# Split 16-bit operands for half of the weighing units, one key distance for every tile, and x1 traffic issued by ScalarE

## The reference, cut to what matters

```python
x = x + attention(ln_channels(x))       # x is (8, 128, 56, 56): 7x7 neighbourhood attention, 16 heads of 8
t = to_tokens(x)
t = t + moe(ln_tokens(t))               # 8 experts, the best 2 by a softmax router, 128 -> 512 -> 128, relu
x = from_tokens(t, x)

# attention, for each pixel and head, over the 49 keys of its clamped 7x7 window:
logits = q . k + rpb[relative row, relative column]
out    = sum(softmax(logits) * v)
y      = out @ proj_w.T + proj_b
```

## Time and profile before

| | us |
|---|---|
| median of 3 runs (3019.34 to 3025.69) | 3022.98 |
| the profiled execution | 3022.68 |
| its span, first to last instruction | 3020.9 |
| busy in the span: PE, PEld | 2688.8, 2395.9 |
| busy in the span: DVE, ACT, POOL | 2269.4, 2114.3, 1583.9 |
| attention | from about 100 to 2250 |
| experts, then combine | from 2250 to 2890, and to the end |

### The profile page before, as it was taken

One profiled execution on the slowest core, in us unless ns is written; L12 is line 12 of the kernel. 1 busy time (PEld: TensorE's weight loads), 2 busy tenths in 40 slices (PEclk: granted clock), 3 DMA queues, 4 the chain that ended last, 5 costly groups with the idle time before them and its releaser, 6 DMA issues. The chain is left out here.

```text
span 3020.9 us, 112796 instructions
## 1 busy us (share of the span) xinstructions
PE 2688.8 (89%) x31346; PEld 2395.9 (79%) x31451; DVE 2269.4 (75%) x12559; ACT 2114.3 (70%) x5724; POOL 1583.9 (52%) x2025
## 2 busy tenths in 40 slices
PE   4789999999999999999999999999939999999733
PEld 2789999899989998999899989999936766776522
DVE  2668888788878887888788868888857888888655
ACT  1567878787878886887787868888847777777500
POOL 2135555455545554555455545555565777777600
PEclk9999999999999999999999999999969999999855
DMA  2665666555546664656566645566645444444399
GB/s 48 153 122 124 129 124 123 112 122 127 126 102 130 124 124 102 130 128 124 101 127 128 129 99 124 125 125 129 132 91 105 97 94 97 97 94 97 101 323 322
DMA packets 714047, 378.50 MB, mean 125 GB/s; under 512 B 422528, under 2 KB 669984, under 8 KB 713504
## 3 DMA queue, kind: packets, MB, share of 16 engines
q1 hardware_dynamic: 660704, 235.97, 40.3%
q10 hardware_dynamic: 24192, 81.67, 9.5%
q0 software_dynamic: 28608, 54.48, 6.1%
HBM read 233.43 MB, written 98.11 MB: 110 GB/s over the span
## 5 line engine op out<-in xcount | busy, mean ns | idle before, releaser
L1061 ACT ACTIVATE pr<-sc,nmx 128x100 f32<-128x100 f32 x3136 | 923.9, 369 | 61.9 <-DVE nmx L678 60.9
L962 POOL TENSOR_TENSOR oml<-om 128x256 f16<-128x256 f32 x784 | 479.6, 612 | 907.3 <-DVE om L708 890.4
L533 PE MATMUL bank<-vwin,pt 100*128 100x65 f32 x6272 | 806.2, 272 | 36.3 <-DVE om L708 28.1
L678 DVE CUSTOM_DVE_ANT_0 sc<-bank,near 128x100 f32<-128x100 f32 x3136 | 633.5, 257 | 253.7 <-PE bank L511 207.8
L533 PEld LDWEIGHTS bank<-vwin,pt 100*128 100x128 f32 x6272 | 773.4, 194 | 54.3 <-ACT pt L1069 39.5
L511 PE MATMUL bank<-kimg,held 128*128 (+2 forms) x9408 | 628.2, 216 | 40.9 <-issue 22.9
L511 PEld LDWEIGHTS bank<-kimg,held 128*128 128x128 bf16 (+1 forms) x9408 | 561.3, 100 | 88.3 <-issue 56.7
L1069 ACT ACTIVATE pt<-bank 100x512 f32<-100x512 f32 x784 | 460.6, 587 | 223.5 <-PE bank L520 208.8
L1367 POOL DMA_INDIRECT yrows<-ye,meta x420 | 449.2, 1070 | 154.6 <-issue 109.8
L930 POOL DMA_INDIRECT xrows<-rows,idx x448 | 433.9, 969 | 114.9 <-issue 75.5
L520 PE MATMUL bank<-cst_sb,pr 128*100 128x128 f32 x3136 | 477.1, 275 | 0.0
(11 more groups left out here) (133 smaller groups left out, 3366.8 us busy)
## 6 DMA issues: line engine op xcount, KB each, us to landing
vwin<-v_pix SPq DMA_DIRECT2D x1120, 60.5 KB
near<-bias_rows ACTq DMA_DIRECT2D x112, 600.0 KB, 4.7
y<-yrows SPq DMA_DIRECT2D x112, 224.0 KB, 4.3
held<-qring SPq DMA_DIRECT2D x896, 14.0 KB
v_pix<-vrow SPq DMA_DIRECT2D x56, 225.8 KB
xin<-in_x SPq DMA_DIRECT2D x56, 224.0 KB
xres<-in_x SPq DMA_DIRECT2D x112, 112.0 KB
x<-xres SPq DMA_DIRECT2D x112, 112.0 KB
```

The costliest lines, as they stand in the source:

```text
L533: mm = pe.matmul(ps_av[m % 2][:, 2 * t + blk, :], pt[:, m % 2, 2 * t + blk, :], vwin[:, st, 2 * u + t, 64 * blk:64 * blk + 65], start=True ...
L678: i = v.tensor_tensor_reduce(out=sc[:, ring(m, par), k, :], in0=ps_s[m % 2][:, k, :], in1=near[:, st, ct, k, :], scale=-1.0, scalar=-MASKE ...
L962: g.tensor_tensor(oml[:, st, u], om[:, st, u], om_h[:, st, u], ALU.subtract).then_inc(s["oml_done"], 1)
L1061: i = a.activation(pr[:, r, k, :], sc[:, r, k, :], ACT.Exp, bias=nmx[:, r, k:k + 1], scale=-1.0)
```

## The change

- `SPLIT` = (0, 3, 4, 5, 7, 10, 12): for these 7 of 14 units `weigh` does 12 matmuls with 16-bit operands instead of 4 in fp32: high x high, high x low, low x high. The high part of `pt` is read in place (every second 16-bit word). The low part `pl` is a subtraction on POOL, `split_t`, after `t_evict`.
- The low part of v is made on DVE by the new `a_v_l` at m = 12, after ACT's eviction of the rows, and stored beside the fp32 row: a pixel has 194 words (VP) instead of 129 (VW) in `v_pix` and `vwin`. `v_out`, for which `store_v` and the next `a_mean` wait, now comes from DVE.
- L_V, L_P, L_H and L_F are one unit later (5, 6, 7, 8), so the folds are at m = 0 and 7 and the projections at m = 2 and 9.
- All tiles take their keys from column 4 t - 3; what lies outside the image is masked, and `kimg` and `v_pix` have 4 zero pixels at either end. A strip's `windows` is ten DMAs of 14 tiles.
- exp is written in place in `sc`; `pr` is gone, and `add_bias` waits for the transposes of four units before.
- `store_x1`, `load_res` and `load_tokens` move from SP's queue to ACT's, at m = 4, 7, 11 and 13. SP's `spread_q` comes ahead of `load_x` and `windows(J, 1)`.
- The router's `gapr` moves from DVE to POOL, and four of the indirect DMAs move by one m.

The diff, cut to its core:

```diff
-L_T, L_V, L_P, L_H, L_F = 3, 4, 5, 6, 7
+L_T, L_V, L_P, L_H, L_F = 3, 5, 6, 7, 8
+SPLIT = (0, 3, 4, 5, 7, 10, 12)
+VP = VW + VW // 2 + 1
-WIN_DMAS = 16 * (KW + 2)
+WIN_DMAS = 16 * KW
...
                     for kr in range(KW):
-                        src = bass.AP(v_pix.tensor, at + (kr * W + 1) * VW, [[VW, KW], [TS * VW, NTILE - 2], [1, VW]])
-                        sp.dma_start(vwin[kr * KW:(kr + 1) * KW, st, 1:NTILE - 1], src).then_inc(s[f"v_in{st}"], 16)
-                    for t, c0 in ((0, 0), (NTILE - 1, W - KW)):
-                        src = bass.AP(v_pix.tensor, at + c0 * VW, [[W * VW, KW], [VW, KW], [1, VW]])
-                        sp.dma_start(vwin[:, st, t], src).then_inc(s[f"v_in{st}"], 16)
+                        src = bass.AP(v_pix.tensor, at + kr * W * VP, [[VP, KW], [TS * VP, NTILE], [1, VP]])
+                        sp.dma_start(vwin[kr * KW:(kr + 1) * KW, st], src).then_inc(s[f"v_in{st}"], 16)
...
 def weigh(J, m, par):
+                    if m in SPLIT:
+                        pe.wait_ge(s["t_out"], len(SPLIT) * J + SPLIT.index(m) + 1)
+                    else:
+                        pe.wait_ge(s["th_done"], n + 1)
...
+                            if m in SPLIT:
+                                p_h, p_l = pt_h[:, m % 2, 2 * t + blk, :], pl[:, m % 2, 2 * t + blk, :]
+                                v_h, v_l = vwin_h[:, st, 2 * u + t, cols], vwin_l[:, st, 2 * u + t, cols]
+                                for k, (a_, b_) in enumerate(((p_h, v_h), (p_h, v_l), (p_l, v_h))):
+                                    mm = pe.matmul(at_, a_, b_, start=k == 0, stop=k == 2)
...
+                def a_v_l(I):
+                    v.wait_ge(s["v_h"], I + 1)
+                    for blk in range(2):
+                        cols = slice(65 * blk, 65 * blk + 64)
+                        i = v.tensor_tensor(vrow_l[:, :, cols],
+                                            ps_a[0:HALF, :].rearrange("p (n c) -> p n c", n=NROW)[:, :, 64 * blk:64 * blk + 64],
+                                            vrow_h[:, :, cols], ALU.subtract)
+                    i.then_inc(s["v_out"], 1)
...
-                LATE_STEPS = {9: a_q_l, 10: a_k_l}
+                LATE_STEPS = {9: a_q_l, 10: a_k_l, 12: a_v_l}
...
+                def split_t(J, m, par):
+                    n = UPP * J + m
+                    g.wait_ge(s["th_done"], n + 1)
+                    g.tensor_tensor(pl[:, m % 2], pt[:, m % 2], pt_h[:, m % 2], ALU.subtract).then_inc(s["t_out"], 1)
...
                             if reached(J, m, L_H):
                                 split_l(*back(J, m, par, L_H))
+                            if reached(J, m, L_T) and (m - L_T) % UPP in SPLIT:
+                                split_t(*back(J, m, par, L_T))
...
+                            elif m == 4:
+                                store_x1(J - 1, 0)
+                            elif m == 7:
+                                load_res(J, 0)
+                            elif m == 11:
+                                store_x1(J - 1, 1)
+                            elif m == 13:
+                                load_res(J, 1)
+                                load_tokens(J - 1, 1 - par)
```

More of the change, by code:

```diff
@@ L383, in body @@
                     more = not (isinstance(J, int) and J == PAIRS - 1)
-                    if not early(J, 1):
-                        store_x1(J - 1, 0)
+                    if more:
+                        spread_q(J + 1, 1 - par)
                     if fetch:
@@ L389, in body @@
                     if more:
[L390 to L394, removed]
                         windows(J + 1, 0, tail)
-                    load_res(J, 1)
-                    if not early(J, 1):
-                        load_tokens(J - 1, 1 - par)
                     if I is not None:
@@ L622, in _ @@
                 v.memset(qexp[:, 1].rearrange("p s t h q -> p (s t h q)"), 0.0).then_inc(s["zeroed"], 1)
+                v.memset(vrow_l[:, :, 64:65], 0.0)
+                v.memset(vrow_l[:, :, VW:VW + 1], 0.0)
                 v.memset(vrow[:, :, 64:65], 1.0).then_inc(s["pad_zero"], 1)
+                for part in range(2):
+                    for col in (0, EDGE + IMG):
+                        i = v.memset(kimg[:, part, col:col + EDGE], 0.0)
+                i.then_inc(s["k_edge"], 1)
                 v.memset(ones_b[:], 1.0)
@@ L743, in rank @@
                     i.then_inc(s["r_top"], 1)
+                    if not early(c, 1):
+                        v.wait_ge(s["r_gapr"], c)
                     v.tensor_tensor(gap[:], top[:, :, 1], top[:, :, 0], ALU.subtract).then_inc(s["r_gap"], 1)
@@ L918, in root @@
                     g.tensor_tensor(nmr[:, par], nm[:], rs[:, par], ALU.mult).then_inc(s["r_nmr"], 1)
+                    g.wait_ge(s["r_gap"], c + 1)
+                    if not early(c, 1):
+                        g.wait_ge(s["r_eg"], 2 * c)
+                    g.tensor_tensor(gapr[:], gap[:], rs[:, par], ALU.mult).then_inc(s["r_gapr"], 1)
                 def scatter(c, par, j, n):
@@ L982, in _ @@
                     split_l(*back(PAIRS, m, PAIRS % 2, L_H))
+                    if m < L_T and (m - L_T) % UPP in SPLIT:
+                        split_t(*back(PAIRS, m, PAIRS % 2, L_T))
                 places_ = sorted(SCATTERS)
@@ L1046, in near_bias, with load_res, store_x1, load_tokens @@
                     a.dma_start(near[:, st].rearrange("p c a k -> p (c a k)"), src).then_inc(s[f"near_in{st}"], 16)
+                def load_res(J, st):
+                    b = J // NPAIR
+                    if not (isinstance(J, int) and J == 0):
+                        a.wait_ge(s[f"x1_store{st}"], 16 * J)
+                    src = bass.AP(x.tensor, b * (C * IMG) + (J % NPAIR) * PAIR + st * STRIP, [[IMG, C], [1, STRIP]])
+                    a.dma_start(xres[:, st, :], src).then_inc(s[f"xres_in{st}"], 16)
+                def store_x1(J, st):
+                    a.wait_ge(s["proj_out"], 2 * J + st + 1)
+                    a.dma_start(x1[:, bass.ds(J * PAIR + st * STRIP, STRIP)], xres[:, st, :])\
+                        .then_inc(s[f"x1_store{st}"], 16)
+                def load_tokens(Q, par):
+                    if not early(Q, 2):
+                        a.wait_ge(s["r_logit"], Q - 1)
+                    a.dma_start(xt[:, par, :], x1[:, bass.ds(Q * PAIR, PAIR)]).then_inc(s[f"r_x{par}"], 16)
                 def exps(J, m, par):
```

75 lines of the change are left out of this document (41 added, 34 removed).

## The result

The changed kernel takes 3196.7 us, the median of 4 runs (3174.72 to 3211.15). The kernel before, on the same chip, takes 3024.34 (3019.34 to 3038.62). The ratio is 1.054 [1.049, 1.059] (these two medians alone give 1.057): 5% slower, where 2906 was forecast and 2990 was the end of the range. The profiled execution took 3174.72, over a span of 3172.9.

What follows compares the result with a forecast made beforehand. PE was taken to bound stretch A of an attention body and DVE stretch B; 18.3 + 16.6 = 34.9 us instead of 37.0, 56 x 2.1 = 118 less 1, so 3022.7 - 117 = 2906 us, range 2855 to 2990.

Steps and rivals of the forecast that it cites:

- the windows' bytes: Window loads: 260 more bytes a piece cost about 15 ns; 2800 pieces on 16 engines, 2.6 us a body.
- Taken as nothing: Longer window loads cost no time: DMA share rises from 21.8 to 24.8 of 34.9 us, with the load more even.
- The cover of `windows(J, 1)`: Strip 1's key loads run from about m=5 to m=8, needed at m=12: 8 us; without it PE waits some 5.
- The mechanism of the gain: Attention body: split units take 0.46 us instead of 0.84, saving 2.7 us for seven; body 37.01 to 34.9 us.
- A: Body stretch from `add_bias` of m=13 to m=7, PE-paced: from 20.1 us to 18.3, bounds 17.4 to 18.9.
- B: Body stretch from `add_bias` of m=7 to m=13, DVE-paced: from 16.91 us to 16.6, bounds 16.2 to 17.4.
- The sum: Whole kernel: 56 bodies gain 2.1 us each, 118 us, less 1 for the start: 3022.7 - 117 = 2906.
- PE's wait for `a_q_l` before `a_k`: In the q, k, v chain of B, PE's wait of 0.53 us gets longer; no new size given.
- Rival 1: Split units' pairs take some 60 ns, a unit 0.72 us: body 36.5, total 2995; chance 0.09.
- Rival 2: `split_t` on POOL makes units 0.3 to 0.5 us late: body 36.9, total about 3015; chance 0.08.
- Rival 3: ACT stands in `load_res(J, 1)` at m=13 until m=11's store lands: at a 10 us landing, 3118; chance 0.09.
- The range: Total time 2855 to 2990 us, leaving out rival 3, most of rival 2 and half of rival 1.

Runs made afterwards that it cites:

- experiments 9 and 10: The changed kernel with window DMAs that write 16 partitions (9, wrong keys) or 5 (10): 3061.02 us, ratio 1.011, and 3306.41 us in one run.
- short pixels: The changed kernel with windows loading only the first 129 of a pixel's 194 words (516 bytes), all matmuls kept: 2933.2 us, ratio 0.967.
- experiment 11: The changed kernel with only strip 1's units split; strip 0 loads 516 bytes of a pixel, strip 1 520: 2915.59 us, ratio 0.9615.

## Why the prediction was wrong, point by point

- **The step that failed: the windows' bytes**, "15 ns more" a piece "on 16 engines 2.6 us ... Taken as nothing". Two terms were mis-sized. The price came from another queue with pieces of 3.4 KB, 17.8 KB/us an engine; a window's piece of 776 bytes took 69.7 ns and one of 516 bytes 47.6, that is 11 KB/us and 22 ns more. And ten engines serve a window DMA, not 16. Together 2800 x 22 / 10 = 6.2 us a body, not 2.6. For the quickest quarter of the pieces 15 ns would have been enough (28 and 38 ns, 10 more); what the price left out is the time that the other pieces lose, more of them the more engines ask (experiments 9 and 10). The page of before had a row that would have told: its queue q1, the windows' own, with packets of all its kinds, moved 235.97 MB at 40.3% of 16 engines in 3020.9 us, 12.1 KB/us.

```profile
q1 hardware_dynamic: 660704, 235.97, 40.3%
```

- **"Taken as nothing"** judged the load by the DMA share, 24.8 of 34.9. But one queue in order, on ten engines for most of its bytes, is full before the share is. By the packet records after 250, SP's queue has packets under way for 28.7 us of a body with short pixels and for 35.4 in the changed kernel. That is 6.7 us more, near the 6.2 above, and 35.4 does not fit a body of 34.9. Why the bodies then average 40.2 is not worked out in full. Two things add to it: SP's own waits (279.0 and 120.1 us), after which the queue can run dry, and the clock. From 1081 to 1083, after PE's 4.74 us of waiting, the granted clock is 0.50, the lower of its two levels (columns as in the earlier trace rows):

```profile
1081.00:1083.00 2.00, 2.00 (x19) 2.00 (x17) 0.00 (x0) 0.60 (x1) 0.00 (x0) 0.50 0.69 175
```

- **The cover of `windows(J, 1)`** was put at 8 us: a start at about m = 5 and an end at m = 8. The start was right, 10.64 us after `a_mean` in the short body. The end was not: the loads run from 1024.07 to 1040.42, 16 us instead of three units of 2.5, so the cover is used up even there, and PE waits 0.62. With short pixels the same loads run from 1028.10 to 1038.43. In the long body the start is 8 us later too, and PE waits 4.74, near the "some 5 us" that the prediction gave for a cover that is gone. What was missing was a rival in which this cover goes, because the queue brings a debt from one body to the next. A short body follows a long one since the wait lets the queue empty.
- **The mechanism of the gain** was right. With short pixels the body is 35.09 (forecast 34.9), A 18.68 (18.3), B 16.41 (16.6), and the split units alone bring 2.06 of it; experiment 11, another kernel, comes to 2915.59, with a body of 34.4 to 34.8. With short pixels 2933 is left, 5.8 of it for the memset, some 21 more than the forecast 2906. The sum took the gain 56 times; 48 bodies have it (36.02 instead of 38.07 on average, with the loop's ends), while the first seven took 237.0 us instead of 233.1 and the stretch behind the last `a_mean` stayed the same. In the body B gained more and A less than forecast: PE's wait for `a_q_l` before `a_k` is 0.62 in the changed kernel, longer than the 0.53 before, as forecast, DVE's wait before `a_q_l` is gone (0.1 was forecast), the one before `a_k_l` is 0.71 to 0.83, about what it was (0.6 was forecast), and `a_v_l` waits 0.23 (0.3 was forecast).
- **Rival 1** (the pairs don't get short) fell: 33 ns a pair, 0.39 us a unit. The Trainium skill (TensorE: Matmul & The Clock Gate, "Back-to-back issue gap") gives about 81 ns for sustained pairs with 128 columns moving. The prediction put that on a unit that moves 65, so its 0.97 us had no ground; the pairs with 100 columns moving already took only 52 to 57 ns.
- **Rival 2** (the chain over POOL) fell: 2.9 us of waiting in 1000 us. (Its sum is 34.9 + 2.1 = 37.0, not 36.9.)
- **Rival 3** (ACT behind a store's landing), the only one on the slower side, fell: 1.004 alone, and in the changed kernel ACT's list has no wait for a store's landing.
- **The range** ended at 2990, since each of its ends came from PE, DVE, POOL and ACT, and none from a queue.

In numbers, of the 240 us between the profiled executions of the changed kernel (3174.7) and the one with short pixels (2934.8): 219.0 lie between the first and last `a_mean`, 23.4 in the last bodies up to the experts, 3.3 behind, and -5.8 is the memset ahead.

What stays open: why a packet takes longer the more engines ask (45, 70, 85 ns at 5, 10 and 16), why the bodies with sixteen partitions are still uneven, and how the 40.2 us of a body come about in full. DMAs that write 20 or more partitions with the right keys weren't tried, nor a third buffer for the keys, with which SP would not wait for `weigh`.

## What to carry to other kernels

Before a transfer grows, add up what its queue does in one body, in order, each entry at the price of its own kind of packet (the queue's bytes over its share in its own row, not another queue's), and on the engines that serve it. A share of 16 engines far below one is no sign of room: ten engines in one stream end at 63%. And where a loop's queue is nearly full, its debt is carried on, so that bodies of uneven length with the same instructions are the thing to look for.

## What the runs showed of the hardware

- A DMA that writes 5, 10 or 16 partitions was served by as many of the 16 engines (q1's share in window stretches: 32.6, 63.3 and, with other entries between, 85.4%), and 90, 104 and 124 GB/s moved. Splitting the DMAs over a second queue moved no more (131 GB/s over the span, against 134), though ACT was held up in that run too.
- On ten engines pieces of 516 bytes took 48 ns on average and pieces of 776 bytes 70, both some 11 KB/us an engine, while a run of 10.9 KB took 819 ns, 13.3 KB/us. In this range the mean goes with the bytes. At least a quarter of the pieces took no more than 28 and 38 ns, for 776 bytes at 5, 10 and 16 partitions alike; the mean rises with the engines that ask (45, 70, 85 ns).
- Twelve matmuls with 16-bit weights of 100 rows and 128 columns and 65 columns moving took 0.39 us, with v's high part read in steps of two 16-bit words; no price of that step shows, since its matmuls (L532) and the ones with the packed low part follow at the same 33 ns.
